# Biases moved from TensorE to VectorE, ScalarE and GpSimd, and expert gates spread over partitions through DRAM, in an FFN with two dense and many routed experts

## The reference

```python
xt = x @ W.T + b + 2 * (x @ A[seq]) @ B[seq]
scores = softmax(xt @ router_w + router_b) + router_bias
gate = top-2 of the best 2 of 4 groups, else 0      # (T, 16)
for e in range(16):
    h = silu(xt @ w1[e] + b1[e]) * (xt @ w2[e] + b2[e])
    y += gate[:, e] * (h @ w3[e] + b3[e])
z = silu(xt @ sw1 + sb1) * (xt @ sw2 + sb2) @ sw3 + sb3
out = x + y + z
```

## Time and profile before

| what | value |
|---|---|
| runs | 129.25, 129.29, 132.18 us |
| median | 129.29 us |
| profiled execution | 129.17 us |
| its span, first to last instruction | 127.3 us |
| granted TensorE clock in all slices | full speed |

### The profile page before, as it was taken

One profiled execution on the slowest core, in us unless ns is written; L12 is line 12 of the kernel. 1 busy time (PEld: TensorE's weight loads), 2 busy tenths in 40 slices (PEclk: granted clock), 3 DMA queues, 4 the chain that ended last, 5 costly groups with the idle time before them and its releaser, 6 DMA issues.

```text
span 127.3 us, 2241 instructions
## 1 busy us (share of the span) xinstructions
PE 123.3 (97%) x815; PEld 102.0 (80%) x815; DVE 86.4 (68%) x195; ACT 47.8 (38%) x84; POOL 19.0 (15%) x33
## 2 busy tenths in 40 slices
PE   6999999999999999999999999999999999999991
PEld 6978867987789787888788889886888888888891
DVE  1659194257879859989999964456715379997631
ACT  1644473697529644007654654241014010000000
POOL 7364005000000020000057000033800000000000
PEclk9999999999999999999999999999999999999999
DMA  3999788669990699549007999994227999332222
GB/s 109 298 322 399 241 351 257 261 221 376 376 346 14 122 192 227 122 143 345 6 0 194 364 278 397 392 359 161 94 82 250 347 396 369 124 127 103 99 88 82
DMA packets 16908, 28.77 MB, mean 226 GB/s; under 512 B 1952, under 2 KB 6432, under 8 KB 16768
## 3 DMA queue, kind: packets, MB, share of 16 engines
q1 hardware_dynamic: 11728, 17.07, 40.5%
q10 hardware_dynamic: 3952, 7.34, 15.9%
q0 software_dynamic: 1216, 4.20, 10.3%
HBM read 19.17 MB, written 9.44 MB: 225 GB/s over the span
## 4 chain that ended last, share of the span: by engine, by line
PE 84%; DMA 6%; SPq 5%; ACT 2%; issue 1%; DVE 0%; ACTq 0%
PE bank L1002 61%; DMA xT_raw<-in_xT 6%; PE bank L1204 6%; PE bank L1061 5%; PE bank L1218 3%; SPq L319 2%; PE bank L1049 2%; PE bank L1279 2%; PE bank L1072 1%; PE bank L1194 1%; PE bank L1035 1%; ACT xT_h L462 1%; PE bank L1109 1%; PE bank L1179 1%; SPq L327 1%
## 5 line engine op out<-in xcount | busy, mean ns | idle before, releaser
L1002 PE MATMUL bank<-xtT_h,w12e_h 128*128 128x512 f32 x32 | 13.1, 409 | 0.0
L1002 PE MATMUL bank<-xtT_h,sw_h 128*128 128x512 f32 x32 | 12.9, 403 | 0.0
L1002 PE MATMUL bank<-xtT_l,sw_h 128*128 128x512 f32 x32 | 12.5, 391 | 0.0
L1002 PE MATMUL bank<-xtT_l,w12e_h 128*128 128x512 f32 x32 | 12.5, 391 | 0.0
L1002 PE MATMUL bank<-xtT_h,w12e_l 128*128 128x512 f32 x32 | 12.5, 391 | 0.0
L1002 PE MATMUL bank<-xtT_h,sw_l 128*128 128x512 f32 x32 | 12.5, 390 | 0.0
L975 DVE SCALAR_TENSOR_TENSOR x_sb<-rows_sb,val,x_sb 128x512 f32<-128x512 f32 x16 | 11.7, 747 | 0.2
L981 DVE TENSOR_TENSOR x_sb<-x_sb,bank 128x512 f32<-128x512 f32 (+1 forms) x9 | 5.6, 625 | 4.8 <-PE bank L1002 4.8
L799 DVE SCALAR_TENSOR_TENSOR heT_sb<-bank,b_dense,sg_sb 128x512 f32<-128x512 f32 x4 | 3.0, 750 | 7.7 <-PE bank L1002 7.7
L1204 PEld LDWEIGHTS bank<-xgT_sb,w_ring 128*128 128x128 f32 x64 | 7.5, 192 | 0.5 <-issue 0.5
L678 DVE TENSOR_TENSOR xT_l<-xT_raw,xT_h 128x512 fp32r<-128x512 f32 (+1 forms) x6 | 5.2, 867 | 3.9 <-ACT xT_h L462 3.8
(11 more groups left out here) (185 smaller groups left out, 292.0 us busy)
## 6 DMA issues: line engine op xcount, KB each, us to landing
y_rows<-zeros ACTq DMA_DIRECT2D x2, 2048.0 KB, 10.6
rows_sb<-y_rows SPq DMA_DIRECT2D x8, 512.0 KB, 7.3
xT_raw<-in_xT SPq DMA_DIRECT2D x8, 256.0 KB, 6.9
xt_rows<-xt_turned SPq DMA_DIRECT2D x8, 256.0 KB, 4.8
w_ring<-in_w_turned SPq DMA_DIRECT2D x4, 512.0 KB, 9.2
x_sb<-in_x SPq DMA_DIRECT2D x1, 2048.0 KB, 14.8
out<-x_sb ACTq DMA_DIRECT2D x7, 256.0 KB, 2.0
condW_raw<-in_condWT ACTq DMA_DIRECT2D x4, 256.0 KB, 5.1
```

Source lines behind the costliest of these rows:

```text
L1002: mm = pe.matmul(out, a[p], b[q], start=(start and n == 0), stop=(stop and n == 2))
```

## The change

- b3 of a block is added when its result leaves PSUM (`copy_y`). The rows of b3 are loaded by SP, spread over partitions, into `b3_ring`, after the weights of the blocks.
- sb3 and the gated b3 of the two dense experts are added to `x_sb` by GpSimd, three additions a tile (`add_biases`): tiles 0 to 3 before the scatters, 4 to 7 after `all_stored`. ScalarE multiplies b3 of a dense expert by the gate of each token (`scale_biases`) into `bias_tmp`; its instructions are placed between others by hand. `add_rows` waits for the tile's three additions.
- x is loaded earlier in SP's queue, before the wait for `eid_ready`.
- VectorE makes the gates of the dense experts alone (`gate_dense`), before `hidden(1)`. TensorE transposes these 16 columns once, before unit 4; ScalarE copies them, stores them to DRAM (`gate_rows`) and loads them back onto all partitions (`gate_row`, 1 MB). `gated` multiplies by this SBUF tile, and stands behind `rest_hidden(0)` and `(1)` for its first time.
- Gone: the tile `gate` with its clearing, eight transposes, two copies, `row_pick`, four `gate_row` products, `b3s_split` with its high and low parts, nine bias products. Some TensorE waits on `unit_gated` become waits on `sh_hidden`, since no bank holds gate rows any more.

The diff, cut to its core:

```diff
@@ sync
-            sp.dma_start(b3s_raw[:], b3s).then_inc(b3s_in, 16)
+            sp.dma_start(sb3_sb[:], sb3.partition_broadcast(P)).then_inc(sb3_in, 16)
...
+            for j in range(DENSE):
+                load_all(b3e_sb[:, j, :], dense[j], b3e_in)
+            sp.wait_ge(cond_done, HALVES_T * KC)
+            sp.dma_start(x_sb[:], x.rearrange("(i p) d -> p i d", p=P)).then_inc(x_in, 16)
             sp.wait_ge(eid_ready, 1)
...
+            sp.wait_ge(sh_up_done, SHARED_UNITS)
+            for s in range(STATIC):
+                load_all(b3_ring[:, s, :], used_experts[s], b3_in[s])
@@ gpsimd
-            pool.wait_ge(logits_done, BATCHES)
-            pool.memset(gate[:], 0.0).then_inc(pool_step, 1)
...
             for b in range(STATIC):
                 gather(b, b, gathered[b])
+            def add_biases(i):
+                if i == 0:
+                    pool.wait_ge(x_in, 16)
+                    pool.wait_ge(sb3_in, 16)
+                pool.tensor_tensor(sums(i), sums(i), sb3_sb[:], ALU.add).then_inc(x_biased, 1)
+                for j in range(DENSE):
+                    pool.wait_ge(x_biased, i * (1 + DENSE) + j + 1)
+                    pool.wait_ge(bias_scaled, i * DENSE + j + 1)
+                    pool.tensor_tensor(sums(i), sums(i), bias_tmp[:, j, :], ALU.add).then_inc(x_biased, 1)
+
+            for i in range(TILES // 2):
+                add_biases(i)
...
             pool.sem_inc(all_stored, 1)
+            for i in range(TILES // 2, TILES):
+                add_biases(i)
@@ scalar
-            act.wait_ge(b3s_in, 16)
-            act.copy(b3s_split[:], b3s_raw[:]).then_inc(b3s_hi, 1)
             gate_silu(3)
             act.wait_ge(slots_done, 1)
+            act.wait_ge(gateT_done, 1)
+            act.copy(gateT[:], bank[6][0:DENSE * TILES, 0:P]).then_inc(gateT_copied, 1)
+            act.wait_ge(gateT_copied, 1)
+            act.dma_start(gate_rows, gateT[:]).then_inc(gate_rows_stored, 16)
             hi_hidden(0)
...
+            def scale_biases(i):
+                if i == 0:
+                    act.wait_ge(b3e_in, 16 * DENSE)
+                    act.wait_ge(gate_ready, 1)
+                for j in range(DENSE):
+                    if i >= 1:
+                        act.wait_ge(x_biased, (i - 1) * (1 + DENSE) + j + 2)
+                    act.activation(bias_tmp[:, j, :], b3e_sb[:, j, :], ACT.Copy, scale=gate_dense[:, j, i:i + 1]
+                                   ).then_inc(bias_scaled, 1)
+
             gate_silu(4)
+            act.wait_ge(gate_rows_stored, 16)
+            act.dma_start(gate_row[:], gate_rows.rearrange("(j i) t -> j (i t)", j=DENSE).partition_broadcast(P)
+                          ).then_inc(gate_row_in, 16)
...
-            for n in range(2):
-                act.wait_ge(gateT_done, n + 1)
-                act.copy(gateT[:, n * 512:(n + 1) * 512], bank[(5, 6)[n]][0:STACK, :]).then_inc(gateT_copied, 1)
             act.wait_ge(w3e_in, 16 * DENSE)
             act.copy(w3e_split[0][:], w3e_raw[:]).then_inc(w3e_hi, 1)
+            scale_biases(0)
             gate_silu(5)
             hi_hidden(3)
             copy_xgT(0)
             copy_xgT(1)
+            scale_biases(1)
             hi_hidden(4)
             silu(0)
             copy_xgT(2)
             silu(1)
             copy_xgT(3)
+            scale_biases(2)
             silu(2)
             hi_hidden(5)
+            scale_biases(3)
             silu(3)
...
             hi_hidden(7)
+            for i in range(TILES // 2, TILES):
+                scale_biases(i)
@@ vector
-                part = unit_part(hid_sb, SHARED_UNITS + v)
-                dve.tensor_tensor(part, part, row_bank(v)[:], ALU.mult).then_inc(unit_gated, 1)
+                dve.tensor_tensor(part, part, gate_row[:, j, n * HALF:(n + 1) * HALF], ALU.mult).then_inc(unit_gated, 1)
...
             dve.engine_nop().then_inc(dense_known, 1)
+            for j in range(DENSE):
+                then(dve.tensor_scalar(is_dense[:, j, :], key[:], key_top[:, j:j + 1], None, ALU.is_equal))
...
+            then(dve.tensor_tensor(dense_sc, sc[:].unsqueeze(1).to_broadcast(by_dense), is_dense[:].unsqueeze(2).to_broadcast(by_dense), ALU.mult))
+            dve.tensor_reduce(gate_dense[:], dense_sc, AX.X, ALU.add).then_inc(gate_ready, 1)
             hidden(1)
...
                 dve.wait_ge(y_done, b + 1)
-                dve.tensor_copy(y_ring[:, b, :], y_bank(b)[:]).then_inc(y_copied, 1)
+                dve.wait_ge(b3_in[b], 16)
+                dve.tensor_tensor(y_ring[:, b, :], y_bank(b)[:], b3_ring[:, b, :], ALU.add).then_inc(y_copied, 1)
...
             def add_rows(i, k):
+                if k == 0:
+                    dve.wait_ge(x_biased, (i + 1) * (1 + DENSE))
@@ tensor
+            pe.wait_ge(sh_hidden, 1)
+            pe.wait_ge(gate_ready, 1)
+            pe.transpose(bank[6][0:DENSE * TILES, 0:P], gate_dense[:].rearrange("p j i -> p (j i)"), ident[:]).then_inc(gateT_done, 1)
             pe.wait_ge(w12e_done, 1)
             pe.wait_ge(sh_hidden, 2)
             dense_up(4, 0)
             dense_up(4, 1)
-            pe.wait_ge(gate_ready, 1)
-            for i in range(TILES):
-                mm = pe.transpose(bank[(5, 6)[i // 4]][0:STACK, (i % 4) * P:(i % 4 + 1) * P], gate[:, i, :], ident[:])
...
-                pe.matmul(out, gateT[:, i * P:(i + 1) * P], b3s_split[:, cols], start=False, stop=False)
```

More of the change, by code:

```diff
@@ L52, in program @@
 def program(nc, x, xT, seq_slot, condWT, cond_b, lora, router_w, router_b, router_bias,
-            w12, w12_turned, b12, w3, b3s, sw12, sb12, sw3, out):
+            w12, w12_turned, b12, w3, b3, sw12, sb12, sw3, sb3, out):
     xt_rows = nc.dram_tensor("xt_rows", (T, DIM), F32, kind="Internal").ap()
+    gate_rows = nc.dram_tensor("gate_rows", (DENSE * TILES, P), F32, kind="Internal").ap()
     y_rows = nc.dram_tensor("y_rows", (K * T + BLOCKS * P, DIM), F32, kind="Internal").ap()
@@ L179, in program @@
         chosen = sb("chosen", [P, TILES, E], BF16)
-        gateT = sb("gateT", [STACK, T], F32R)
+        is_dense = sb("is_dense", [P, DENSE, E])
+        gate_dense = sb("gate_dense", [P, DENSE, TILES])
+        gateT = sb("gateT", [DENSE * TILES, P])
         padded_i = sb("padded_i", [P, E], I32)
@@ L239, in program @@
         hs_hi, hs_done, sw3_hi, sw3_done = sem("hs_hi"), sem("hs_done"), sem("sw3_hi"), sem("sw3_done")
-        b3s_in, b3s_hi, b3s_done, gate_ones = sem("b3s_in"), sem("b3s_hi"), sem("b3s_done"), sem("gate_ones")
+        sb3_in, b3e_in, x_biased, bias_scaled = sem("sb3_in"), sem("b3e_in"), sem("x_biased"), sem("bias_scaled")
+        b3_in = [sem(f"b3_in{s}") for s in range(STATIC)]
         zeros_set, rows_zeroed, dense_known = sem("zeros_set"), sem("rows_zeroed"), sem("dense_known")
         w12e_hi, w12e_done, w3e_hi, w3e_done = sem("w12e_hi"), sem("w12e_done"), sem("w3e_hi"), sem("w3e_done")
-        row_pick_ready, gate_row_done, unit_gated = sem("row_pick_ready"), sem("gate_row_done"), sem("unit_gated")
+        gate_rows_stored, gate_row_in, unit_gated = sem("gate_rows_stored"), sem("gate_row_in"), sem("unit_gated")
         used_ready, blk_hit_ready, blk_tok_ready, slot_row_ready = (
@@ L359, in _ @@
                 load_one(w3_ring[:, s, :], w3, e, w3_in[s])
-            sp.wait_ge(cond_done, HALVES_T * KC)
-            sp.dma_start(x_sb[:], x.rearrange("(i p) d -> p i d", p=P)).then_inc(x_in, 16)
+                used_experts.append(e)
+            sp.wait_ge(sh_up_done, SHARED_UNITS)
+            for s in range(STATIC):
+                load_all(b3_ring[:, s, :], used_experts[s], b3_in[s])
             by_tile = y_rows[0:K * T, :].rearrange("(k i p) d -> k p i d", k=K, p=P)
@@ L878, in _ @@
             dve.engine_nop().then_inc(eid_ready, 1)
[L879 to L882, removed]
             hidden(2)
@@ L947, in one @@
                 dve.wait_ge(more_y, n)
-                dve.tensor_copy(y_ring[:, 0, :], y_bank(0)[:]).then_inc(more_copied, 1)
+                dve.wait_ge(more_b3, 16 * n)
+                dve.tensor_tensor(y_ring[:, 0, :], y_bank(0)[:], b3_ring[:, 0, :], ALU.add).then_inc(more_copied, 1)
             more_blocks(dve, used, one)
@@ L1104, in dense_up @@
                     mm.then_inc((sh_gate_done, sh_up_done)[m], 1)
-            def gate_row(v):
-                j, n = v // HALVES_T, v % HALVES_T
-                pe.matmul(row_bank(v)[:], row_pick[:, j, :], gateT[:, n * HALF:(n + 1) * HALF], start=True, stop=True
-                          ).then_inc(gate_row_done, 1)
             pe.wait_ge(zeros_ready, 1)
@@ L1225, in _ @@
             used = blocks_used(pe)
-            pe.wait_ge(unit_gated, 1)
+            pe.wait_ge(sh_hidden, 5)
             up(0)
@@ L1311 @@
     w12 = w12.reshape(E, KC, P, 2 * INTER).transpose(0, 2, 1, 3).reshape(E, P, W12)
-    b3s = np.concatenate([np.asarray(L0_ffn_eb3), np.asarray(L0_ffn_sb3)[None]], axis=0)
-    b3s = np.tile(np.pad(b3s, ((0, 32 - E - 1), (0, 0))), (3, 1))
     laid = {
@@ L1332 @@
```

(1 more changed line is left out.)

60 lines of the change are left out of this document (21 added, 39 removed).

## The result

The change makes the kernel slower: 137.51 us as the median of 4 runs (136.03 to 138.34) beside 129.46 for the kernel before, a ratio of 1.054 with a 95% interval of 1.050 to 1.058. The forecast was 132.9.

What follows compares the result with a forecast made beforehand. TensorE was taken to bound the kernel before (84% of the chain), VectorE to end the changed one: 103 + 11.7 + 11 x 1.15 = 127.35, plus 1.53 and 3.98, gives 132.9 us; range 126.2 to 137.2.

Steps and rivals of the forecast that it cites:

- TensorE's net gain: Transposes, gate rows and bias products removed from TensorE save 3.7 us, less a 0.9 wait before unit 4: 2.8 us.
- gate load lands: The 1 MB gate load through DRAM lands at 72.3 to 79.7; free up to 79.1, late end 0.6, taken as 0.
- first `down`: TensorE's first `down` in the block stage, at 81.81 before, starts 0.4 earlier.
- one addition, alone: One GpSimd addition of 128x512 takes 1.15 us, the middle between 0.77 and 1.54.
- GpSimd done with its first half: GpSimd's 12 additions ahead of the scatters go at ScalarE's pace and are done near 90.8.
- row loads issued: After four scatters and a landing of about 2.5, the row loads start near 98.5 instead of 95.17.
- first `add_rows`: The first pair of rows lands about 4.5 after the row loads start, so VectorE's tail begins at 103.
- adds of the last sums; around and after: VectorE's adds of the last TensorE sums, 1.53 us; then 3.98 from the last add to the measured time.
- rival C: Additions of 1.5 or more delay GpSimd's first half and hold the fourth `down`: 140 us; chance 0.10 with the tail's worst.
- The tail's own sum: In the tail VectorE's 16 two-input additions, 11.7 us, and GpSimd's 11 of 1.15 exclude each other, from 103 to 127.35.
- Rival A: VectorE and GpSimd run side by side in the tail and TensorE sets the end: 126.4 us; chance 0.27.
- The block bias: b3 added as blocks leave PSUM: `copy_y(0)` some 2 us late at worst; cost taken as 0, bad end 1.5.

Runs made afterwards that it cites:

- experiment 4: The change with GpSimd's 24 additions replaced by memsets about as long that read nothing, shared bias and dense b3 left out: 129.44 us, ratio 1.002.
- experiment 5: The change with VectorE adding the routed rows of tiles 0 to 6 into TensorE's PSUM bank, all biases kept: 131.85 us, ratio 1.020 to the kernel before.
- experiment 3: The change without GpSimd's additions and without the gates' store and load through DRAM: 126.91 us, ratio 0.981 to the kernel before.
- experiment 1: The change without GpSimd's additions of the shared bias and the dense experts' b3: 129.26 us, ratio 0.998 to the kernel before.
- experiment 2: The change without the gates' store and load through DRAM, the hidden part multiplied by itself: 134.2 us, ratio 1.039 to the kernel before.
- experiment 10: The change with rows added in PSUM, gates in two loads, another order and x loaded at 40 us, every bias kept: 129.55 us, ratio 0.997.
- experiment 11: The change with nothing but x loaded at 40 us: 137.6 us, ratio 1.059 to the kernel before.

## Why the prediction was right in kind and too small

The forecast named the mechanism, and it holds: the two engines shut each other out (1223 ns against 747; gone with memsets; gone with PSUM operands), VectorE ends the kernel and not TensorE, and the time goes up. The Trainium skill, "SBUF — State Buffer", section "Who interferes with whom", says this of both directions, and that a VectorE instruction with one SBUF input and a GpSimd instruction that only writes are outside of it. The runs agree with each of these (1223 ns and 2.31 us for the one direction, 1.7 instead of 1.28 us for the other; 749 beside the memsets of experiment 4; 755 in experiment 5 and 686 for `copy_y` in the change).

The forecast of 132.9 was 3.1 us under the profiled execution and 4.6 under the median, which lies 0.3 above the range. By its own steps:

| step | forecast | measured |
|---|---|---|
| TensorE's net gain | 2.8 us | 2.7 (experiment 3, last add) |
| `hidden(1)` ends; unit 4 starts | 65.4 | 65.43; 65.58 |
| gate load issued | 70.3 | 70.33 |
| gate load lands | 72.3 to 79.7, free until 79.1 | 81.0 |
| first `down` | 81.4 | 83.81 |
| one addition, alone | 1.15 | 1.28 |
| GpSimd done with its first half | 90.8 | 94.08 |
| row loads issued | 98.5 | 101.78 |
| first `add_rows` | 103 | 107.79 |
| from there to the end of the last `add_rows` | 24.35 | 22.65 |
| adds of the last sums; around and after | 1.53; 3.98 | 1.27; 4.32 |

Forecast 103 + 24.35 + 1.53 + 3.98 = 132.9; measured 107.79 + 22.65 + 1.27 + 4.32 = 136.03. The tail started 4.8 late, and two steps failed ahead of it, of which the second mostly follows from the first.

- "So a landing up to 79.1 is free and the late end costs 0.6. I take 0." The gate load landed 10.7 us after its issue, past the bound of 9.4, which came from loads a quarter to a half of its size. It also made the ring loads later, and TensorE waited 0.86 for one of them. `times_up(0)` ended at 83.71 instead of 79.97, and the first `down` started 2.4 later than forecast. With store and load left out, the ring loads take 8.4 and 2.0 to 2.2 us are gone (experiments 1 to 3). The step was mis-sized because it asked only how late the load may be and not what it takes from the loads beside it.
- "So GpSimd goes at ScalarE's pace and is done near 90.8." It was done at 94.08, 3.3 later. It did go at ScalarE's pace, but that pace hung on the gates too, which the forecast did not follow: `hi_hidden(4)` waited 2.14 us for `gated(0)` in ScalarE's order, and `scale_biases(2)` stands behind a copy that waits for the late first `down`. With store and load of the gates left out, GpSimd was done at 91.44, 2.6 earlier, with its additions as long. The other 0.6 fits the length of the additions: 1.28 alone, but 1.5 to 1.7 where they met VectorE's subtractions, which the sum for this half left out. Memsets, which nothing lengthens, were done at 93.32, 0.8 earlier. ScalarE in turn waited 0.95 for GpSimd before it could scale the rows that stand ahead of `silu(3)`, and TensorE waited 0.95 for the fourth `down`: rival C's place and mechanism, in a small form and already at 1.28, below the 1.5 put down as its condition. All this moved the scatters, the row loads (101.78 for 98.5) and with them the start of the tail.

The other 1.5 us of the late start are the landing of the first rows, 6.0 us behind their issue (107.79 - 101.78) and not 4.5. With the memsets it was 5.0, without the gates 5.7; what lengthened it was not separated.

The tail's own sum was 1.7 us too long, although the addition is dearer than taken. With both engines busy, a pair of one addition and one `add_rows` took about 1.7 us (VectorE came round to the next tile after 3.40, for two of each), less than 1.28 + 0.68 = 1.96: the second to come does not wait for the whole of the first. And GpSimd had finished by 125.02, so that VectorE's last additions ran at their old pace (1.53 for two). It was luck that this error stood against the late start: without it the forecast would have been 4.8 us short and not 3.1.

From TensorE's gain alone (experiment 3) to the change it is 0.073 of the ratio, 9.4 us: 2.2 for the gates and 7.3 for the additions. Experiment 5 gives back 4.4 of these, but that does not make the other 2.9 the block stage's. TensorE's last product ends at 125.53 in the change, 125.47 with memsets and 125.17 without additions, so they cost TensorE about 0.4 in the block stage, and experiment 5 has a lag of VectorE of its own. By experiment 4 some 6.8 us of the 7.3 are the two engines shutting each other out, nearly all of it in the tail.

Rival A, side by side, is what experiment 5 makes of the tail, at the price of other operands. In the change as it stands no row bears A out. The block bias was priced right: `copy_y(0)` waited 1.03 for its rows, and in experiment 3 a wait of 2.4 at the same place cost the end nothing (in experiment 4 a wait of 3.0 there stood on the chain). TensorE's last product ended at 125.53 and not near 122, because the block stage gave back more than TensorE had gained; with the gates' store and load left out it ended at 122.51.

Of the versions tried, none that keeps every bias beats the kernel before by more than its interval; experiment 10, at 0.997, comes nearest.

## What to carry to other kernels

Work that leaves a full engine for an idle one is paid on a third, if that one and the idle one hold each other up, as VectorE and GpSimd do here: before moving elementwise work to GpSimd, list VectorE's instructions with two SBUF inputs in the same stretch, and see whether one of their inputs can stay in PSUM. Where that sum is made for one stage, make it for every stage in which the two meet. A load that is "in time" still takes its time from the loads beside it: price it by the stage's loads, and by its size, and follow its delay into every engine that has work behind it in order.

## What the runs showed that was not expected

- Groups of memsets, 1.25 us each, in the places of the additions, cost VectorE nothing: `add_rows` took 749 ns beside 748 with an idle GpSimd.
- A GpSimd addition of 128x512 f32 took 1.28 us alone, two inputs and one output. The Trainium skill, "GPSIMD Engine Reference", section 3.1, leads to an estimate of 1.11; the measured 1.28 decides.
- An 8 KB store to DRAM took 3.9 us in the change, with a 2 MB load of x under way, and 1.4 us with that load out of the way (experiments 10 and 11).
